# Node-weight products in units of four PSUM banks, with the full-array and half-array passes in alternating order

## The chip, the cores and the metric

One core of one Trainium2 chip runs the whole kernel. The metric is the device time in microseconds (us). The engines have one instruction queue each and meet through semaphores: PE (matmuls, with its weight loads shown apart as PEld), DVE (vector), ACT (scalar) and POOL (general-purpose). PSUM, where the matmuls write, has eight banks of 128 x 512 float32.

## The reference, cut to what matters

Four layers of a graph network run one after the other on a state of 8 batches x 1024 nodes x 64 features, each followed by a residual sum and a layer norm. The change lies in the third:

```python
    def _L2_gnn_ref(x, A, embedding, weight, bias):
        w = jnp.einsum('nd,dkio->nkio', embedding, weight)     # (1024, 3, 64, 64)
        b = jnp.einsum('nd,do->no', embedding, bias)
        As = [jnp.eye(N, dtype=x.dtype), A]
        As.append(2.0 * (A @ As[-1]) - As[-2])
        x_g = jnp.einsum('knm,bmc->bnkc', jnp.stack(As, 0), x)
        out = jnp.einsum('bnki,nkio->bno', x_g, w)
        return out + b
...
    x = _layernorm(x + _L2_gnn_ref(x, adj, L2_gnn_embedding, L2_gnn_weight, L2_gnn_bias), axis=-1)
```

Each node has weights of its own, a mix of D = 16 weight matrices by its embedding. The kernel does not build them. It multiplies the three inputs x, A x and A A x by all 16 matrices and then sums the 16 results of 64 columns, each scaled by the node's embedding value.

## The kernel before

The nodes lie in NT = 8 tiles of 128. For each tile t the work goes in units j. A unit is one matmul target: some batches times one half (dh) of the 16 matrices, which is 8 matrices x 64 = 512 columns, one PSUM bank for each batch. Before, a unit has two batches and so two banks, and a tile has UNITS = 8 units, of which the function `products` (L1646 to L1665) makes one at a time.

Every value is split into a high and a low part in a reduced float format, so one float32 product is three passes (high x high, high x low, low x high). The inputs x and A x of a batch stand together as 128 rows: they need three **full-array** passes for each bank (KH, KL against WH, WL: L1654 to L1656). The third input, A A x, has only 64 rows for each batch (GH, GL: L1664). Two batches, in the upper and in the lower half of the array, run as a pair of **half-array** passes at the same time. So a unit before is 6 full passes followed by 3 pairs of half passes.

The full passes need x and A x turned (features on the partitions). `turn(t)` (L1637) has PE transpose the 8 batches into two banks, 8 transposes from the buffer XX. ACT copies the two banks to KH (L1490, `turned`), DVE subtracts KH from the banks for KL (L1551, `low_parts`), and ACT then fills XX for the next tile (L1475, L1476, `inputs`).

What a unit leaves in its banks is taken out by two engines in turn. DVE's `accumulate` adds five of the eight groups of 64 columns, scaled, into X3, one chained instruction after the other (L1564). Then, `act.wait_ge(acc_step, DV * (u + 1))`, ACT's `scaled` writes the other three, scaled, to the ring SY (L1503). POOL sums the SY entries (L1432, L1435) and adds that sum to X3 once per tile (L1441, `combine`). PE's `banks_free` waits until ACT has taken out the unit that last used the same banks.

The order is written out by hand in the list `rounds`, which all engines follow: the turn of tile t + 1 stands between units 3 and 4 of tile t. Banks go round in four pairs, so PE is up to three units ahead of the one whose banks it takes back:

```python
        def pair_of_banks(t, j):
            at = 2 * (rounds.index((t, j)) % 4)
            return slice(at, at + 2)
```

Between the units ACT and DVE also do the layer norm of finished tiles: DVE takes statistics (L140) and makes scales, POOL makes the reciprocal roots (L163), ACT's `apply_norm` scales and shifts groups of 64 columns (L1510, two of them after a unit) and `next_high` (L1514) and DVE's `next_low` (L1577) make the inputs of the last layer. That layer's matmuls (L1705) begin when all 8 tiles are normed.

Of the kernel before, what the change touches and what calls it, by code (L numbers as in the profile page):

```python
# [9 lines left out]
ALU = mybir.AluOpType  # L10
# [6 lines left out]
F = 64  # L17
# [45 lines left out]
def program(nc, x_nat, x_tr, adj_tr, h_nat, h_tr, consts, weights, w01, w2, emb_bias, out):  # L63
    ctx = ExitStack()
    with ctx:
# [1044 lines left out]
        with nc.Block() as block:  # L1110
# [264 lines left out]
        kT_ready, k_h, k_l, y_ready, acc_step, sy_ready, yp_step, x3_sum = (  # L1375
            sem(s) for s in ("kT_ready", "k_h", "k_l", "y_ready", "acc_step", "sy_ready", "yp_step", "x3_sum"))
# [7 lines left out]
        UNITS = 2 * BP  # L1384
        SYS = 8
        SY = sb("SY", [P, SYS, 2 * F])
# [8 lines left out]
        def pair_of_banks(t, j):  # L1395
            at = 2 * (rounds.index((t, j)) % 4)
            return slice(at, at + 2)
# [9 lines left out]
        with nc.Block() as block:  # L1407
            @block.gpsimd
            def _(pool):
# [14 lines left out]
                def add_scaled(t, q):  # L1424
                    acc = YP[t % 2][:, tile(q)]
                    for i in range(1, 2 * DA):
                        n = 2 * DA * (BP * t + q) + i
                        pool.wait_ge(sy_ready, n + 1)
                        if i == 1:
                            if t >= 2:  # L1430
                                pool.wait_ge(x3_sum, t - 1)
                            ins = pool.tensor_tensor(acc, SY[:, (n - 1) % SYS, :], SY[:, n % SYS, :], ALU.add)  # L1432
                        else:
                            pool.wait_ge(yp_step, yp_steps(n - 1))
                            ins = pool.tensor_tensor(acc, acc, SY[:, n % SYS, :], ALU.add)  # L1435
                        ins.then_inc(yp_step, 1)

                def combine(t):
                    pool.wait_ge(acc_step, DV * unit(t + 1, 0))
                    pool.wait_ge(yp_step, yp_steps(2 * DA * BP * (t + 1) - 1))  # L1440
                    pool.tensor_tensor(X3[:, t, :], X3[:, t, :], YP[t % 2], ALU.add).then_inc(x3_sum, 1)  # L1441
# [7 lines left out]

                init(0)  # L1450
                for t in range(NT):
                    for q in range(BP):
                        add_scaled(t, q)
                        if q == 1:
                            for i, (first, n) in enumerate(NORMS):
                                if first + n == t:
                                    scales(i)
                        if q == 2 and t + 1 < NT:
                            init(t + 1)
                    combine(t)  # L1460
# [3 lines left out]
            def _(act):  # L1464
# [7 lines left out]
                def inputs(t):  # L1472
                    if t >= 1:
                        act.wait_ge(kT_ready, t)
                    act.activation(XX[:, :, 0, :], groups(X2[:, t, :]), ACT.Copy).then_inc(xx_ready, 1)  # L1475
                    act.activation(XX[:, :, 1, :], groups(XA[:, t, :]), ACT.Copy).then_inc(xx_ready, 1)  # L1476

                inputs(0)
                for i in range(2 * BP):
                    act.wait_ge(a2_ready, i + 1)  # L1480
                    act.activation(GH[:, i // 2, (i % 2) * HALF:(i % 2 + 1) * HALF], PS[:, 2 + i % 2, :], ACT.Copy,
                                   scale=2.0).then_inc(g_h, 1)
# [12 lines left out]
                def scaled(t, j):  # L1495
                    u = unit(t, j)
                    act.wait_ge(acc_step, DV * (u + 1))
                    for d in range(DV, DH):
                        n = DA * u + d - DV
                        if n >= SYS:  # L1500
                            act.wait_ge(yp_step, yp_steps(n - SYS))
                        e = W_EMB + t * D + (j % 2) * DH + d
                        act.activation(groups(SY[:, n % SYS, :]), PS[:, pair_of_banks(t, j), d * F:(d + 1) * F], ACT.Copy,  # L1503
                                       scale=WT[:, e:e + 1]).then_inc(sy_ready, 1)
# [11 lines left out]
                for t, j in rounds:  # L1516
                    if j is None:
                        turned(t)
                    else:
                        scaled(t, j)  # L1520
                        for i in range(3):
                            k = unit(t, j) - (16 * i + 22)
                            if 0 <= k < 8:
                                apply_norm(i, 2 * k, 2)
                            if k in (4, 8):
                                next_high(2 * i + k // 4 - 1)
# [6 lines left out]
            def _(dve):  # L1533
# [7 lines left out]
                for i in range(2 * BP):  # L1541
                    dve.wait_ge(g_h, i + 1)
                    c = slice((i % 2) * HALF, (i % 2 + 1) * HALF)
                    dve.scalar_tensor_tensor(GL[:, i // 2, c], PS[:, 2 + i % 2, :], 2.0, bits(GH[:, i // 2, c]),
                                             ALU.mult, ALU.subtract).then_inc(g_l, 1)

                def low_parts(t):
                    at = pair_of_banks(t, None).start
                    for h in range(2):
                        dve.wait_ge(k_h, 2 * t + h + 1)  # L1550
                        dve.tensor_tensor(KL[:, t % 2, 4 * h:4 * h + 4, :], PS[:, at + h, :].rearrange("p (b c) -> p b c", c=P),  # L1551
                                          bits(KH[:, t % 2, 4 * h:4 * h + 4, :]), ALU.subtract).then_inc(k_l, 1)

                def accumulate(t, j):
                    u, q, dh = unit(t, j), j // 2, j % 2
                    acc = groups(X3[:, t, tile(q)])
# [3 lines left out]
                    for d in range(DV):  # L1560
# [3 lines left out]
                        dve.scalar_tensor_tensor(acc, PS[:, pair_of_banks(t, j), d * F:(d + 1) * F], WT[:, e:e + 1], acc,  # L1564
# [14 lines left out]
                for t, j in rounds:  # L1579
                    if j is None:  # L1580
                        low_parts(t)
                        continue
                    accumulate(t, j)
                    if t >= 1 and j == 1:
                        statistics(t - 1)
                    if j == 2:
# [3 lines left out]
                    for i in range(3):  # L1590
                        k = unit(t, j) - (16 * i + 22)
                        if k in (6, 9):
                            next_low(2 * i + k // 3 - 2)
# [6 lines left out]
            def _(pe):  # L1600
# [8 lines left out]
                for i in range(2 * BP):  # L1609
                    q, c = i // 2, slice((i % 2) * HALF, (i % 2 + 1) * HALF)  # L1610
                    acc = PS[:, 2 + i % 2, :]
# [16 lines left out]
                def banks_free(t, j):  # L1628
                    i = rounds.index((t, j))
                    if i < 4:  # L1630
                        return
                    was_t, was_j = rounds[i - 4]
                    if was_j is None:
                        pe.wait_ge(k_l, 2 * was_t + 2)
                    else:
                        pe.wait_ge(sy_ready, DA * (unit(was_t, was_j) + 1))

                def turn(t):
                    at = pair_of_banks(t, None).start
                    banks_free(t, None)  # L1640
# [4 lines left out]

                def products(t, j):  # L1646
                    q, dh, r = j // 2, j % 2, t % 2
                    at = pair_of_banks(t, j).start
                    c = slice(dh * DH * F, (dh + 1) * DH * F)
                    banks_free(t, j)  # L1650
                    pe.wait_ge(k_l, 2 * t + q // 2 + 1)
                    for par in range(2):
                        b, acc = 2 * q + par, PS[:, at + par, :]
                        pe.matmul(acc, KH[:, r, b, :], WH[:, 0, c], start=True, stop=False, skip_group_check=True)  # L1654
                        pe.matmul(acc, KH[:, r, b, :], WL[:, 0, c], start=False, stop=False, skip_group_check=True)  # L1655
                        pe.matmul(acc, KL[:, r, b, :], WH[:, 0, c], start=False, stop=False, skip_group_check=True)  # L1656
                    if t == 0 and dh == 0:
                        pe.wait_ge(g_l, 2 * q + 1)
                    if t == 4 and j == 0:
                        pe.wait_ge(g_l, 2 * BP)  # L1660
                    for g, w in ((GH, WH), (GH, WL), (GL, WH)):
                        for par in range(2):
                            rows = slice(F * par, F * par + F)
                            ins = pe.matmul(PS[:, at + par, :], g[rows, q, tile(t)], w[rows, 1, c],  # L1664
                                            start=False, stop=(g is GL), skip_group_check=True)  # L1665
# [186 lines left out]
```

## Time and profile before

| | |
|---|---|
| timed runs, median of 3 | 905.51 us (902.73 to 907.22) |
| the profiled execution: its own time | 904.9 us |
| its span in the trace | 903.1 us |
| PE busy | 754.8 us, 84% of the span |
| DVE, ACT, POOL busy | 479.8, 345.5, 289.3 us |
| mean granted clock of PE | 0.907 of full speed |
| stretch of the units, from the first product to the last | 626.84 to 791.3 us of the span |

A matmul's duration in the trace covers its way through the array, and the next one starts before it ends. The time that a matmul costs is therefore read from one start to the next. "Idle before" in brackets is the time for which the engine stood still ahead of a row, and the name behind the arrow is what it waited for.

### The profile page before, as it was taken

The numbers are of one execution on the slowest core, as the hardware profiler recorded it, in microseconds if no ns is written. First come the engines' busy times: TensorE is split into PE (matmuls) and PEld (weight loads), VectorE is DVE, ScalarE is ACT, GpSimd is POOL, SyncE is SP. The second block draws the span as 40 slices with busy tenths as digits, with TensorE's granted clock in tenths as the row PEclk, the third lists the DMA queues.
The fourth block names the chain that finished last, engine by engine and source line by source line (L and its number), as shares of the span: only waits on it lengthen the run. The fifth ranks groups of instructions, "written<-read, shape, count | busy, mean of one in ns | idle before, by whom it ended". The sixth has DMA issues, their size and how long they took to land. (4 is left out here: it accounts for less than half of the span.)

```text
span 903.1 us, 10528 instructions
## 1 busy us (share of the span) xinstructions
PE 754.8 (84%) x3510; PEld 495.1 (55%) x3518; DVE 479.8 (53%) x1158; ACT 345.5 (38%) x724; POOL 289.3 (32%) x337
## 2 busy tenths in 40 slices
PE   3966977888898459899898993999999999939990
PEld 3646765666565358433232322787666666628880
DVE  1494254777357831245464666312778878820165
ACT  1741213545463121346353542222445564642110
POOL 0440001445446320001003149000556576730055
PEclk9967995999997579989998996899999999969995
DMA  8200011000000000000000001000000000000013
GB/s 277 70 24 1 1 32 62 2 1 0 1 1 1 0 1 1 1 0 1 1 0 1 0 5 45 1 1 1 1 1 0 1 1 1 1 0 1 1 24 70
DMA packets 12952, 14.39 MB, mean 16 GB/s; under 512 B 9680, under 2 KB 9680, under 8 KB 12896
## 3 DMA queue, kind: packets, MB, share of 16 engines
q1 hardware_dynamic: 11408, 11.61, 4.1%
q10 hardware_dynamic: 1488, 2.06, 0.7%
q8 instruction: 32, 0.52, 0.2%
q14 instruction: 24, 0.20, 0.1%
HBM read 11.57 MB, written 2.10 MB: 15 GB/s over the span
## 5 line engine op out<-in xcount | busy, mean ns | idle before, releaser
L1564 DVE SCALAR_TENSOR_TENSOR arena<-PS,WT,arena 128x128 f32<-128x128 f32 x320 | 111.2, 350 | 20.2 <-PE PS L1664 9.3
L1329 DVE TENSOR_REDUCE arena<-PS 128x1 f32<-128x1024 f32 x64 | 75.6, 1219 | 79.7 <-PE PS L1165 79.7
L1252 ACT ACTIVATE arena<-PS,arena 128x1024 f32<-128x1024 f32 x64 | 70.8, 1109 | 74.9 <-DVE arena L1329 74.9
L1503 ACT ACTIVATE SY<-PS,WT 128x128 f32<-128x128 f32 x192 | 56.5, 365 | 78.3 <-DVE arena L1564 78.3
L163 POOL TENSOR_TENSOR LN_Y<-LN_V,CN 128x16 f32<-128x16 f32 (+1 forms) x17 | 51.0, 2998 | 104.8 <-DVE LN_V L155 104.8
L1165 PE MATMUL PS<-arena 64*128 64x512 f32 x256 | 79.2, 636 | 4.6 <-ACT arena L1252 2.4
L1272 POOL TENSOR_TENSOR arena<-arena 128x128 f32<-128x128 f32 x32 | 12.9, 403 | 191.6 <-DVE arena L1333 191.6
L1183 PE MATMUL PS<-arena 128*64 128x512 f32 x256 | 64.2, 625 | 1.2 <-POOL arena L1272 1.1
L1654 PE MATMUL PS<-WH,KH 128*128 128x512 f32 x128 | 57.1, 446 | 1.4 <-DVE KL L1551 1.4
L1165 PEld LDWEIGHTS PS<-arena 64*128 64x128 f32 x256 | 28.9, 190 | 52.3 <-issue 33.4
L1655 PE MATMUL PS<-WL,KH 128*128 128x512 f32 x128 | 50.5, 395 | 0.0
L1656 PE MATMUL PS<-WH,KL 128*128 128x512 f32 x128 | 49.9, 390 | 0.0
L1705 PE MATMUL PS<-ADJH,NH 128*128 128x512 f32 x128 | 33.7, 407 | 15.2 <-PEq L1407 15.2
L1183 PEld LDWEIGHTS PS<-arena 128*64 128x64 f32 x256 | 16.3, 141 | 46.8 <-issue 44.4
L908 POOL TENSOR_TENSOR arena<-arena,CC 128x512 f32<-128x512 f32 x24 | 25.0, 1042 | 43.5 <-DVE arena L787 43.5
L1654 PEld LDWEIGHTS PS<-WH,KH 128*128 128x128 f32 x128 | 24.0, 187 | 25.3 <-issue 12.5
L140 DVE BATCH_NORM_STATS2 LN_ST<-arena 128x6 f32<-128x64 f32 x256 | 35.2, 209 | 3.4 <-POOL arena L1441 3.0
L1041 PE MATMUL PS<-arena,WT 128*128 128x512 f32 x64 | 36.0, 716 | 0.0
L1705 PEld LDWEIGHTS PS<-ADJH,NH 128*128 128x128 f32 x128 | 24.6, 197 | 20.5 <-issue 15.7
L1435 POOL TENSOR_TENSOR AGBD<-AGBD,SY 128x128 f32<-128x128 f32 x64 | 29.5, 461 | 18.7 <-ACT SY L1503 11.1
L895 POOL TENSOR_TENSOR HPL<-arena,HPH 128x512 fp32r<-128x512 f32 x8 | 10.2, 1279 | 78.6 <-ACT HPH L825 78.6
L1435 POOL TENSOR_TENSOR YP<-YP,SY 128x128 f32<-128x128 f32 x64 | 30.0, 469 | 16.5 <-ACT SY L1503 8.5
(263 smaller groups left out, 1608.0 us busy)
## 6 DMA issues: line engine op xcount, KB each, us to landing
arena<-in_adj_tr SPq DMA_DIRECT2D x8, 512.0 KB, 8.3
arena<-in_x_tr SPq DMA_DIRECT2D x4, 512.0 KB, 9.3
arena<-in_x_nat SPq DMA_DIRECT2D x1, 2048.0 KB, 8.3
out<-arena SPq DMA_DIRECT2D x8, 256.0 KB, 3.0
arena<-in_w SPq DMA_DIRECT2D x2, 512.0 KB, 4.1
WT<-in_weights ACTq DMA_DIRECT2D x1, 739.0 KB, 8.6
arena<-in_h_tr ACTq DMA_DIRECT2D x2, 256.0 KB, 10.8
CN<-in_consts ACTq DMA_DIRECT2D x1, 507.0 KB, 5.2
```

Of the source, the lines that this page charges most:

```text
L163: pool.tensor_tensor(LN_Y[:, at:at + n], LN_V[:, at:at + n], CN[:, C_NEGH:C_NEGH + n], ALU.pow).then_inc(ln_rstd, 1)
L1165: ins = pe.matmul(banks("S", 2 * i + par)[:, half, :], KT[q % 2][r, tile(m)], QT[q % 2][r, c], start=True, stop=True)
L1183: ins = pe.matmul(PS[r, 6 + half, :], AVN[:, i % RING, par, :], EF[2 * (i % RING) + par][:, c], start=(m == 0), stop=(m == NT - 1), skip_g ...
L1252: act.activation(EF[2 * (i % RING) + par], banks("S", 2 * i + par).rearrange("p a c -> p (a c)"), ACT.Exp, bias=NMX[:, i, par:par + 1], ac ...
L1329: dve.tensor_reduce(NMX[:, i, par:par + 1], banks("S", 2 * i + par), AX.XY, ALU.max, negate=True).then_inc(max_ready, 1)
L1435: ins = pool.tensor_tensor(acc, acc, SY[:, n % SYS, :], ALU.add)
L1503: act.activation(groups(SY[:, n % SYS, :]), PS[:, pair_of_banks(t, j), d * F:(d + 1) * F], ACT.Copy, scale=WT[:, e:e + 1]).then_inc(sy_rea ...
L1564: dve.scalar_tensor_tensor(acc, PS[:, pair_of_banks(t, j), d * F:(d + 1) * F], WT[:, e:e + 1], acc, ALU.mult, ALU.add).then_inc(acc_step, 1)
L1654: pe.matmul(acc, KH[:, r, b, :], WH[:, 0, c], start=True, stop=False, skip_group_check=True)
L1655: pe.matmul(acc, KH[:, r, b, :], WL[:, 0, c], start=False, stop=False, skip_group_check=True)
L1656: pe.matmul(acc, KL[:, r, b, :], WH[:, 0, c], start=False, stop=False, skip_group_check=True)
L1705: pe.matmul(acc, NH[:, m, tile(q)], ADJH[:, m, c], start=(m == 0), stop=False, skip_group_check=True)
```

## The change

A unit becomes four batches and four banks, so that a tile has four units (UNITS = BP = 4) and the banks go round in two sets, banks 0 to 3 for even units and 4 to 7 for odd ones. Each instruction of DVE, ACT and POOL that takes out or sums a unit handles 256 columns in place of 128, in half as many instructions. The ring SY keeps its size in bytes: 4 entries of twice the width. Even units do the 12 full passes first and then the 6 pairs of half passes, odd units the half passes first. The turn of tile t + 1 stands between units 1 and 2 of tile t and goes to banks 2 and 3, which unit 2 is about to fill. ACT copies both banks to XX in one instruction (semaphore k_raw), makes KH from XX in a second, and the subtraction for KL moves to POOL. XX for the next tile but one is filled after unit 3. `apply_norm` does four groups after a unit.

```diff
-        UNITS = 2 * BP
-        SYS = 8
-        SY = sb("SY", [P, SYS, 2 * F])
+        UNITS = BP
+        SYS = 4
+        SY = sb("SY", [P, SYS, 4 * F])
...
-            rounds += [(t, j) for j in range(4)] + ([(t + 1, None)] if t + 1 < NT else []) + [(t, j) for j in range(4, UNITS)]
+            rounds += [(t, j) for j in range(2)] + ([(t + 1, None)] if t + 1 < NT else []) + [(t, j) for j in range(2, UNITS)]
...
+        def four_banks(t, j):
+            at = 4 * (j % 2)
+            return slice(at, at + 4)
+
+        turn_banks = slice(2, 4)
...
+                def low_parts(t):
+                    pool.wait_ge(k_h, t + 1)
+                    pool.tensor_tensor(KL[:, t % 2, :, :], XX[:, :, :, :].rearrange("p b k f -> p b (k f)"), bits(KH[:, t % 2, :, :]), ALU.subtract).then_inc(k_l, 1)
...
+                low_parts(0)
                 init(0)
                 for t in range(NT):
...
+                    add_scaled(t, 0)
+                    for i, (first, n) in enumerate(NORMS):
+                        if first + n == t:
+                            scales(i)
+                    if t + 1 < NT:
+                        low_parts(t + 1)
+                        init(t + 1)
+                    add_scaled(t, 1)
                     combine(t)
...
                 def turned(t):
-                    at = pair_of_banks(t, None).start
+                    raw = XX[:, :, :, :].rearrange("p b k f -> p b (k f)")
                     act.wait_ge(kT_ready, t + 1)
                     if t >= 2:
                         act.wait_ge(y_ready, unit(t - 1, 0))
-                    for h in range(2):
-                        act.activation(KH[:, t % 2, 4 * h:4 * h + 4, :], PS[:, at + h, :].rearrange("p (b c) -> p b c", c=P),
-                                       ACT.Copy).then_inc(k_h, 1)
-                    if t + 1 < NT:
-                        inputs(t + 1)
+                    act.activation(raw, PS[:, turn_banks, :].rearrange("p a (b c) -> p (a b) c", c=P), ACT.Copy).then_inc(k_raw, 1)
+                    act.wait_ge(k_raw, t + 1)
+                    act.activation(KH[:, t % 2, :, :], raw, ACT.Copy).then_inc(k_h, 1)
...
                         scaled(t, j)
+                        if j == 3 and t + 2 < NT:
+                            inputs(t + 2)
                         for i in range(3):
-                            k = unit(t, j) - (16 * i + 22)
-                            if 0 <= k < 8:
-                                apply_norm(i, 2 * k, 2)
+                            k = unit(t, j) - (8 * i + 11)
+                            if 0 <= k < 4:
+                                apply_norm(i, 4 * k, 4)
...
-                def banks_free(t, j):
...
+                def banks_free(u):
+                    if u >= 2:
+                        pe.wait_ge(sy_ready, DA * (u - 1))
...
+                def two_terms(t, j, first):
+                    g, dh = j // 2, j % 2
+                    c = slice(dh * DH * F, (dh + 1) * DH * F)
+                    pe.wait_ge(k_l, t + 1)
+                    for i in range(4):
+                        if j == 2 and i == 2 and t + 1 < NT:
+                            pe.wait_ge(k_raw, t + 2)
+                        b, acc = 4 * g + i, PS[:, four_banks(t, j).start + i, :]
+                        passes = ((KH, 0, WH), (KH, 0, WL), (KL, 0, WH))
+                        for n, (x, k, w) in enumerate(passes):
+                            ins = pe.matmul(acc, x[:, t % 2, b, :], w[:, k, c], start=(first and n == 0),
+                                            stop=(not first and n == 2), skip_group_check=True)
+                    return ins
...
                 def products(t, j):
...
+                    banks_free(unit(t, j))
+                    if j % 2 == 0:
+                        two_terms(t, j, True)
+                        ins = third_term(t, j, False)
+                    else:
+                        third_term(t, j, True)
+                        ins = two_terms(t, j, False)
                     ins.then_inc(y_ready, 1)
```

`third_term` holds the half passes of L1664 in the same pairs, for p = 0 and 1. Nothing outside this stage is changed.

On PE, in order of issue, this is the turn of tile 1 inside tile 0 before: the end of unit 3, the turn and the beginning of unit 4. L1654 to L1656 are full passes, L1664 pairs of half passes, L1643 the 8 transposes.

```order
L1654 MATMUL PS<-WH,KH 128x512
L1655 MATMUL PS<-WL,KH 128x512
L1656 MATMUL PS<-WH,KL 128x512
L1664 MATMUL PS<-WH,GH 128x512 x2
L1664 MATMUL PS<-WL,GH 128x512 x2
L1664 MATMUL PS<-WH,GL 128x512 x2
L1643 MATMUL PS<-CN,XX 128x128 x8
L1654 MATMUL PS<-WH,KH 128x512
L1655 MATMUL PS<-WL,KH 128x512
L1656 MATMUL PS<-WH,KL 128x512
```

And this is the same place now: the last full passes of unit 1, the turn (L1641), and the first of unit 2, whose two first banks take the six full passes (L1654) shown here; the wait for k_raw stands behind the sixth.

```order
L1654 MATMUL PS<-WL,KH 128x512
L1654 MATMUL PS<-WH,KL 128x512
L1641 MATMUL PS<-CN,XX 128x128 x8
L1654 MATMUL PS<-WH,KH 128x512
L1654 MATMUL PS<-WL,KH 128x512
L1654 MATMUL PS<-WH,KL 128x512
L1654 MATMUL PS<-WH,KH 128x512
L1654 MATMUL PS<-WL,KH 128x512
L1654 MATMUL PS<-WH,KL 128x512
```

The half passes have gone from both sides of the turn. Six full passes of unit 2 now stand between the turn and the two banks that hold its result.

On ACT, this is the beginning of the stage before: the copies to KH for tile 0 (L1490), XX for tile 1, four units of SY (12 instructions), and then the turned inputs of tile 1.

```order
L1490 ACTIVATE KH<-PS 128x512 x2
L1475 ACTIVATE XX<-arena 128x8x64
L1476 ACTIVATE XX<-arena 128x8x64
L1503 ACTIVATE SY<-PS,WT 128x128 x12
L1490 ACTIVATE KH<-PS 128x512 x2
```

And now: two copies in a chain (L1499, L1501), XX for tile 1, two units of SY (L1511, 6 instructions), and the copies for tile 1.

```order
L1499 ACTIVATE XX<-PS 128x1024
L1501 ACTIVATE KH<-XX 128x1024
L1485 ACTIVATE XX<-arena 128x8x64
L1486 ACTIVATE XX<-arena 128x8x64
L1511 ACTIVATE SY<-PS,WT 128x256 x6
L1499 ACTIVATE XX<-PS 128x1024
L1501 ACTIVATE KH<-XX 128x1024
```

The copy that empties the turn's banks (L1499) still stands behind all SY instructions of the unit that PE finished just before the turn, and these are now unit 1 of four banks where they were unit 3 of two.

## Rows read from the trace of the kernel before

**Rows 1.** Windows: busy time by engine, instructions in brackets, from first product to last

```profile
core 0: us, PE busy (x) PEld busy (x) DVE busy (x) ACT busy (x) POOL busy (x), PEclk, DMA share, GB/s
626.84:791.30 164.46, 164.45 (x824) 104.01 (x824) 132.62 (x419) 87.24 (x269) 100.16 (x177) 1.00 0.00 1
```

**Rows 2.** Timeline of PE, unit 3 of tile 0 and the turn of tile 1

```profile
start us, us, engine line op out<-in xcount [idle before <-releaser]
634.27 0.50 PE L1654 MATMUL PS<-WH,KH 128*128 128x512 f32 x1
634.61 0.40 PE L1655 MATMUL PS<-WL,KH 128*128 128x512 f32 x1
634.85 0.39 PE L1656 MATMUL PS<-WH,KL 128*128 128x512 f32 x1
...
635.86 0.50 PE L1664 MATMUL PS<-WH,GH 64*128 64x512 f32 x2
636.19 0.40 PE L1664 MATMUL PS<-WL,GH 64*128 64x512 f32 x2
636.43 0.39 PE L1664 MATMUL PS<-WH,GL 64*128 64x512 f32 x2
636.75 1.09 PE L1643 MATMUL PS<-CN,XX 128*128 128x128 f32 x8
637.60 0.47 PE L1654 MATMUL PS<-WH,KH 128*128 128x512 f32 x1
```

**Rows 3.** Timelines of DVE and ACT behind that same unit 3

```profile
636.87 1.89 DVE L1564 SCALAR_TENSOR_TENSOR arena<-PS,WT,arena 128x128 f32<-128x128 f32 x5 [0.59 <-PE PS L1664]
...
638.79 0.88 ACT L1503 ACTIVATE SY<-PS,WT 128x128 f32<-128x128 f32 x3 [1.59 <-DVE arena L1564]
639.56 0.60 ACT L1490 ACTIVATE KH<-PS 128x512 fp32r<-128x512 f32 x1
```

**Rows 4.** Groups by line and shape, whole span: count, busy us, mean ns

```profile
L1564 DVE SCALAR_TENSOR_TENSOR arena<-PS,WT,arena 128x128 f32<-128x128 f32 x320 | 111.2, 350 | 20.2 <-PE PS L1664 9.3
L1544 DVE SCALAR_TENSOR_TENSOR GL<-PS,GH 128x512 fp32r<-128x512 f32 x8 | 5.5, 691 | 22.9 <-ACT GH L1481 22.9
L1503 ACT ACTIVATE SY<-PS,WT 128x128 f32<-128x128 f32 x192 | 56.5, 365 | 78.3 <-DVE arena L1564 78.3
L355 ACT ACTIVATE arena<-PS,WT 128x256 f32<-128x256 f32 x2 | 0.8, 470 | 0.0
L1738 ACT ACTIVATE arena<-PS 128x1024 f32<-128x1024 f32 x8 | 8.2, 1024 | 57.9 <-PE PS L1710 57.9
L1435 POOL TENSOR_TENSOR AGBD<-AGBD,SY 128x128 f32<-128x128 f32 x64 | 29.5, 461 | 18.7 <-ACT SY L1503 11.1
L1421 POOL TENSOR_TENSOR arena<-arena,BO 128x512 f32<-128x512 f32 x8 | 10.3, 1288 | 31.6 <-ACT XX L1476 31.6
L283 POOL TENSOR_TENSOR ADJL<-arena,ADJH 128x1024 fp32r<-128x1024 f32 x8 | 19.7, 2486 | 43.5 <-ACT ADJH L295 43.5
```

**Rows 5.** Windows around idle stretches of PE, with the granted clock (PEclk)

```profile
436.57:439.37 2.80, 0.01 (x1) 0.00 (x0) 2.75 (x4) 2.28 (x4) 0.40 (x1) 1.00 0.00 0
439.37:444.80 5.43, 5.43 (x12) 1.45 (x12) 0.00 (x0) 1.13 (x2) 0.00 (x0) 0.69 0.00 0
479.60:482.44 2.84, 0.04 (x1) 0.00 (x1) 2.78 (x4) 2.29 (x4) 2.25 (x4) 0.88 0.00 0
482.44:489.20 6.76, 6.76 (x12) 1.94 (x12) 0.00 (x0) 1.13 (x2) 0.30 (x1) 0.54 0.01 2
625.40:626.84 1.44, 0.03 (x1) 0.00 (x1) 1.26 (x3) 1.37 (x3) 0.00 (x0) 1.00 0.00 0
```

**Rows 6.** Timeline of PE, the turn of tile 0 and the first product

```profile
624.39 1.03 PE L1643 MATMUL PS<-CN,XX 128*128 128x128 f32 x8
626.84 0.50 PE L1654 MATMUL PS<-WH,KH 128*128 128x512 f32 x1 [1.41 <-DVE KL L1551]
```

**Rows 7.** Timelines of POOL and ACT at the end of the stage

```profile
793.71 1.64 POOL L1435 TENSOR_TENSOR YP<-YP,SY 128x128 f32<-128x128 f32 x3 [1.06 <-ACT SY L1503]
795.50 1.26 POOL L1441 TENSOR_TENSOR arena<-arena,YP 128x512 f32<-128x512 f32 x1
...
794.03 2.76 ACT L1510 ACTIVATE arena<-arena,LN_B,LN_Y 128x64 f32<-128x64 f32 x8
```

More of the change, by code:

```diff
@@ L1392, in program, with four @@
         for t in range(NT):
[L1393 to L1397 removed]
+            rounds += [(t, j) for j in range(2)] + ([(t + 1, None)] if t + 1 < NT else []) + [(t, j) for j in range(2, UNITS)]
[3 more added lines that the diff above has]
+        turn_banks = slice(2, 4)
+        def four(g):
+            return slice(g * 4 * F, (g + 1) * 4 * F)
         def unit(t, j):
@@ L1422, in init, with add_scaled @@
                                        BO[:, t:t + 1, :].broadcast_to([P, B, F]), ALU.add).then_inc(x3_init, 1)
-                def add_scaled(t, q):
-                    acc = YP[t % 2][:, tile(q)]
+                def low_parts(t):
+                    pool.wait_ge(k_h, t + 1)
+                    pool.tensor_tensor(KL[:, t % 2, :, :], XX[:, :, :, :].rearrange("p b k f -> p b (k f)"), bits(KH[:, t % 2, :, :]), ALU.subtract).then_inc(k_l, 1)
+                def add_scaled(t, g):
+                    acc = YP[t % 2][:, four(g)]
                     for i in range(1, 2 * DA):
-                        n = 2 * DA * (BP * t + q) + i
+                        n = 2 * DA * (2 * t + g) + i
                         pool.wait_ge(sy_ready, n + 1)
@@ L1502, in scaled @@
                         e = W_EMB + t * D + (j % 2) * DH + d
-                        act.activation(groups(SY[:, n % SYS, :]), PS[:, pair_of_banks(t, j), d * F:(d + 1) * F], ACT.Copy,
+                        act.activation(groups(SY[:, n % SYS, :]), PS[:, four_banks(t, j), d * F:(d + 1) * F], ACT.Copy,
                                        scale=WT[:, e:e + 1]).then_inc(sy_ready, 1)
@@ L1543, in _ @@
                     c = slice((i % 2) * HALF, (i % 2 + 1) * HALF)
-                    dve.scalar_tensor_tensor(GL[:, i // 2, c], PS[:, 2 + i % 2, :], 2.0, bits(GH[:, i // 2, c]),
+                    dve.scalar_tensor_tensor(GL[:, i // 2, c], PS[:, 4 + i % 2, :], 2.0, bits(GH[:, i // 2, c]),
                                              ALU.mult, ALU.subtract).then_inc(g_l, 1)
[L1547 to L1552, printed above, removed]
                 def accumulate(t, j):
-                    u, q, dh = unit(t, j), j // 2, j % 2
-                    acc = groups(X3[:, t, tile(q)])
+                    u, g, dh = unit(t, j), j // 2, j % 2
+                    acc = groups(X3[:, t, four(g)])
                     if j == 0:
@@ L1580, in _ @@
                     if j is None:
-                        low_parts(t)
                         continue
                     accumulate(t, j)
-                    if t >= 1 and j == 1:
+                    if t >= 1 and j == 0:
                         statistics(t - 1)
-                    if j == 2:
+                    if j == 1:
                         for i, (first, n) in enumerate(NORMS):
@@ L1590, in _ @@
                     for i in range(3):
-                        k = unit(t, j) - (16 * i + 22)
-                        if k in (6, 9):
-                            next_low(2 * i + k // 3 - 2)
+                        k = unit(t, j) - (8 * i + 11)
+                        if k in (2, 4):
+                            next_low(2 * i + k // 2 - 1)
                 statistics(NT - 1)
@@ L1626, in _ @@
                 pe.wait_ge(wl_ready, 2)
-                def banks_free(t, j):
[L1629 to L1636, printed above, removed]
+                def banks_free(u):
+                    if u >= 2:
+                        pe.wait_ge(sy_ready, DA * (u - 1))
                 def turn(t):
-                    at = pair_of_banks(t, None).start
-                    banks_free(t, None)
+                    at = turn_banks.start
+                    banks_free(unit(t, 0) - 2 if t else 0)
                     pe.wait_ge(xx_ready, 2 * t + 2)
@@ L1644, in turn @@
                     ins.then_inc(kT_ready, 1)
-                def products(t, j):
[L1647 to L1665, printed above, removed]
@@ new lines, in third_term @@
+                def third_term(t, j, first):
+                    g, dh = j // 2, j % 2
+                    c = slice(dh * DH * F, (dh + 1) * DH * F)
+                    if t == 0 and j < 2:
+                        pe.wait_ge(g_l, 2 * BP if j else 3)
+                    for p in range(2):
+                        for n, (x, w) in enumerate(((GH, WH), (GH, WL), (GL, WH))):
+                            for par in range(2):
+                                rows = slice(F * par, F * par + F)
+                                ins = pe.matmul(PS[:, four_banks(t, j).start + 2 * p + par, :], x[rows, 2 * g + p, tile(t)], w[rows, 1, c],
+                                                start=(first and n == 0), stop=(not first and n == 2), skip_group_check=True)
+                    return ins
```

28 lines of the change are left out of this document (11 added, 17 removed).

## The prediction

> **What bounds the kernel now.** I read the page's slices first: around 630 to 790 us of the span PE is busy all the time and its clock is full. One window over the stage says it exactly [rows 1]: from the first product at 626.84 to the last at 791.3 us PE is busy for 164.45 of 164.46 us at a granted clock of 1.00, DVE for 132.6, ACT for 87.2, POOL for 100.2. So here only PE's own issue counts, and the next question is what it spends its time on. The timeline of one unit answers that [rows 2]: the unit begins at 634.27, the turn at 636.75, so a unit takes 2.48 us. Within it a full pass follows a full pass after 0.24 us or a little less (634.61, 634.85), and one pair of half passes the other after 0.24 (636.19, 636.43). Yet the first pass of each kind is followed only after 0.33 to 0.34 us (634.27 to 634.61, 635.86 to 636.19), and the last half pair is followed by the turn after 0.32. Nine slots of 0.234 us are 2.11 us. The 0.37 that is left belongs to the two changes of kind, 0.185 us each. Check: 64 units of 2.48 and 7 turns of 0.85 (636.75 to 637.60) are 164.7 us, against 164.5 in the trace. There are no other waits to win.
>
> The second thing to read is what stands behind a unit [rows 3]. The turn is issued at 636.75, DVE starts at 636.87, its five chained instructions take 1.89 us, ACT starts 0.03 us later, its three take 0.88, and the copy of the turned inputs starts 0.11 us before they end, at 639.56. Before, this costs PE nothing: it has four pairs of banks, and while ACT is still at unit 3 it works on units 4 and 5.
>
> **The change, part by part.** *Fewer changes of kind.* A unit is now 12 full passes and 6 pairs of half passes, 18 slots, and since the order alternates only one change is left in it: 18 x 0.234 + 0.185 = 4.40 us [rows 2]. Thirty-two of them are 140.8 us. The turn now stands between full passes; I keep 0.85 us for it and 0.08 for the slower pass behind it, 6.5 us for seven. Together 147.3 us, which is **17.2 us less**. Bounds: the passes and their count are the same as before, so nothing beyond the changes of kind can be saved.
>
> *Wider instructions of DVE, ACT and POOL.* None of these shapes stands in this stage, so I take them between rows [rows 4]. DVE: 350 ns at 128 columns, 691 at 512; on the straight line 464 at 256, and up to 484 if the first 128 columns cost more in overhead; I take 475. The chain's pitch grows as the duration does, from 1.89 us for five to **2.52** (2.45 to 2.56). ACT: a scaled copy of 256 columns took 470 ns against 365 for 128, so three take 0.88 + 3 x 0.105 = **1.20 us**. POOL: 461 ns and 1288 at 512 give 737. A unit is then out of its banks 0.2 + 2.52 + 0.03 + 1.20 + 0.05 = 4.0 us after PE has ended it. (The 0.2 is the 0.12 of rows 3 plus the longer way of an odd unit's last full pass.) PE is by then 4.0 us into the next unit of 4.40, so in plain units there is no wait, with 0.4 us to spare. DVE has 4.40 - 2.52 = 1.9 us between units, and the statistics and scales that stand there are shorter.
>
> *The turn is the exception, and I expect the gain to go there.* Let PE end unit 1 of a tile at time 0. It makes the turn until 0.85 and the six full passes of unit 2's first two banks until 0.85 + 0.08 + 6 x 0.234 = 2.33. Then it stands before banks 2 and 3, which hold the turned inputs. ACT can only copy them after unit 1's SY, and that waits for DVE's chain: 0.2 + 2.52 + 0.03 + 1.20 - 0.11 = 3.84, plus the copy of 1024 columns, 1.02 us [rows 4], plus 0.05 = 4.92. So PE waits for **2.6 us** (the profile will call it about 2.4, since the last pass still runs). Behind PE stands everything: the rest of unit 2 and all later units. Seven turns: 18.2 us. At two of them (tiles 3 and 5) `apply_norm` with four groups stands on ACT between SY and the copy. Eight groups took 2.76 us [rows 7], so four add about 1.35 us each time, 2.7 us. Bounds for one wait: with DVE and ACT at their present 1.89 and 0.88 us it is 1.65, and with the upper ends of the durations 2.7. The Trainium skill, TensorEngine Tiling (Array Packing), section PSUM Bottleneck, warns that packing speeds up PE but not the emptying of PSUM. That speaks against this change, and the wait above is what it would look like.
>
> *The start.* Before, PE waits 1.41 us between the turn of tile 0 and the first product at 626.84 [rows 6]. Now ACT copies 1024 columns from the turn's end at 625.47 to 626.5, then again to KH until 627.6, and then POOL subtracts 128 x 1024, 2.49 us by the nearest row (the same operation and shape, L283) [rows 4]: first product at 630.15, **3.3 us later**. In later tiles the same subtraction is hidden by units 2 and 3: KH is ready at 4.92 + 1.02 = 5.9 us after unit 1, and PE comes to the next tile at 4.92 + 3.0 + 4.40 = 12.3. Of these 6.4 us the subtraction takes 2.49; what is left, 3.9, must hold POOL's backlog, the reciprocal roots above all, and anything over it would go onto PE.
>
> *The end.* After the last product DVE's chain is 0.63 us longer, the first SY entry 0.1, and POOL's three additions, 1.64 us now [rows 7], take 2 x 0.87 + 0.74 = 2.47. X3's last sum comes **1.6 us later** after the last product, and all of the last layer's start hangs on it.
>
> Without the clock: -17.2 + 18.2 + 2.7 + 3.3 + 1.6 = **+8.6 us**, which makes 913.5 from the profiled execution's 904.9.
>
> *The clock.* Before, PE never stops in this stage. Now it stops eight times. What a stop of that length does is seen elsewhere in the trace [rows 5]: after 2.80 us of idle PE was granted 0.69 of its clock over the next 5.43 us, a loss of 1.7 us at full clock; after another of 2.84, 0.54 over 6.76 us, a loss of 3.1; after 1.44 us, at the start of this very stage, nothing. These are its two levels, 1.2 and 2.4 GHz, in a mix. My stops (five of 2.4, two of 3.8, one of 4.7 us) are nearer to the ones that cost. I take 1.7 us for six of the eight, **10 us**; the bounds are 0 and 8 x 3.1 = 25. That makes **923.5 us**. The profiled execution lies 0.6 us under the median of the timed runs, which I leave as it is.
>
> **The rivals.** *The clock holds.* The stops at the turns are a little shorter than those that cost, and PE is dense on both sides. Then only the start and the two long ones cost: 913.5 to 917. For it: the 1.44 us stop. Against: two of two stops of 2.8 us. The Trainium skill, TensorE: Matmul & The Clock Gate, section Why this matters for your kernels, sets its limit for idle gaps above my 2.4 us and so is on this rival's side; the 2.80 us rows are already below that limit and fell.
>
> *The wait at the turn is short.* If the time of a DVE or ACT instruction were mostly fixed, so that 256 columns cost what 128 do, the wait would be 1.65 us, seven of them 11.6, the end only 0.8 longer, and the stops so near to 1.44 that the clock holds: 904.9 - 17.2 + 11.6 + 2.7 + 3.3 + 0.8 = 906, **not slower** by a measurable amount. The place is DVE's chain and ACT's SY at the seven turns; it decides from a wait of (17.2 - 2.7 - 3.3 - 1.6) / 7 = 1.4 us downwards for faster. Against it: 512 columns take twice the time of 128 in rows 4.
>
> *The clock falls hard.* If each stop costs like the second, 3.1 us, the sum is 913.5 + 25 = 938.
>
> **How the numbers follow.** Clock falls at most stops, 918 to 931: 0.58. Clock holds, 911 to 917: 0.22. Short wait, 899 to 910: 0.12, a third of it below 901. Harder fall or another wait, above 931: 0.08. The range leaves out the last two cases: 910 to 931. A measurement of this kernel can tell about 0.5%, 4.5 us, from no change: faster (under 901) 0.04, within (901 to 910) 0.08, slower 0.88.
>
> **What would show it.** In the profile after, PE stands still once in each of seven tiles, in front of the seventh full pass of unit 2, for about 2.4 us, twice 3.8, released by ACT's copy of 1024 columns. The passes of L1654 and L1667 must show 0.234 us from start to start and one change of 0.18 in each unit; a plain unit must last 4.40. DVE's five must take about 2.5 us, ACT's three 1.2. The first product must come 5.8 us after the turn of tile 0 begins. The granted clock must show falls behind some of the stops. Wrong would be: waits in front of other units (the 0.4 us to spare is not there), a DVE instruction far from 475 ns, or a clock that stays at 1.00.

## The result, and the profile after

The changed kernel takes 923.66 us (median of 4 runs, 922.41 to 925.05), the kernel before 904.12 us (median of 4, 902.12 to 907.22): its time is put at 1.0204 times the one before, 95% interval 1.0176 to 1.0232 (the two medians alone give 1.0216). It is slower clear of the noise, by about 2%. The profiled execution took 923.8 us with a span of 922.0; before it was 904.9 and 903.1.

The page of the changed kernel, its head:

```profile
span 922.0 us, 10016 instructions
PE 749.9 (81%) x3518; PEld 509.1 (55%) x3518; DVE 438.7 (48%) x982; ACT 336.7 (37%) x628; POOL 293.8 (32%) x265
```

PE is busy for 5 us less than before and the kernel is 19 us longer: PE's work did shrink, and PE stands still instead. Where it does is seen on the timeline of PE. These are the first product, then unit 1's last pass, the turn and unit 2 of tile 0 (in [rows 2] the turn at 636.75 had a product 0.85 us behind it and no stop), and then the first rows behind the stops of tiles 3 and 6:

```profile
630.05 0.80 PE L1654 MATMUL PS<-WH,KH 128*128 128x512 f32 x1 [4.62 <-POOL KL L1431]
...
641.05 0.39 PE L1654 MATMUL PS<-WH,KL 128*128 128x512 f32 x1
641.28 1.03 PE L1641 MATMUL PS<-CN,XX 128*128 128x128 f32 x8
642.07 0.47 PE L1654 MATMUL PS<-WH,KH 128*128 128x512 f32 x1
...
643.31 0.40 PE L1654 MATMUL PS<-WH,KL 128*128 128x512 f32 x1
646.25 0.50 PE L1654 MATMUL PS<-WH,KH 128*128 128x512 f32 x1 [2.54 <-ACT XX L1499]
...
712.37 0.80 PE L1654 MATMUL PS<-WH,KH 128*128 128x512 f32 x1 [3.91 <-ACT XX L1499]
...
780.70 0.50 PE L1654 MATMUL PS<-WH,KH 128*128 128x512 f32 x1 [2.60 <-ACT XX L1499]
```

There are seven such stops, one in each tile but the last, five of 2.54 to 2.60 us and two (tiles 3 and 5) of 3.91 and 3.90, 20.7 us together; each delays PE by 0.16 more than is shown, since the last pass still runs. The same place on DVE and ACT:

```profile
641.48 2.56 DVE L1569 SCALAR_TENSOR_TENSOR arena<-PS,WT,arena 128x256 f32<-128x256 f32 x5 [1.69 <-PE PS L1654]
...
644.08 1.21 ACT L1511 ACTIVATE SY<-PS,WT 128x256 f32<-128x256 f32 x3 [3.05 <-DVE arena L1569]
645.16 1.03 ACT L1499 ACTIVATE XX<-PS 128x1024 f32<-128x1024 f32 x1
```

The chain is as long as its parts: 2.56 us on DVE, 1.21 on ACT, 1.03 for the copy, where [rows 3] had 1.89 and 0.88 and nobody waited. The groups that answer to [rows 4]:

```profile
L1569 DVE SCALAR_TENSOR_TENSOR arena<-PS,WT,arena 128x256 f32<-128x256 f32 x160 | 77.4, 484 | 88.0 <-PE PS L1667 64.3 <-PE PS L1654 16.1 <-DVE LN_ST L140 2.9
L1511 ACT ACTIVATE SY<-PS,WT 128x256 f32<-128x256 f32 x96 | 38.6, 473 | 101.2 <-DVE arena L1569 101.2
L1444 POOL TENSOR_TENSOR AGBD<-AGBD,SY 128x256 f32<-128x256 f32 x32 | 23.6, 738 | 22.0 <-ACT SY L1511 18.2 <-POOL AGBD L1444 0.4
L1431 POOL TENSOR_TENSOR KL<-XX,KH 128x1024 fp32r<-128x1024 f32 x8 | 19.0, 2377 | 65.0 <-ACT KH L1501 65.0
```

DVE lost 34 us of work in this stage and gained nothing by it: it now waits for PE, and PE at each turn waits for ACT's copy, which stands behind DVE's own chain. The windows behind the start and behind the stops show the clock. Its column is the third from the end (1.00 is 2.4 GHz, half of it 1.2):

```profile
630.05:635.60 5.55, 5.55 (x14) 3.96 (x16) 0.00 (x0) 1.13 (x2) 1.18 (x1) 0.52 0.01 3
690.20:693.60 3.40, 3.40 (x18) 2.71 (x20) 0.57 (x2) 0.00 (x0) 3.32 (x3) 0.53 0.00 0
712.37:717.50 5.13, 5.13 (x18) 3.66 (x20) 0.00 (x0) 1.03 (x1) 3.60 (x2) 0.52 0.01 3
758.09:762.00 3.91, 3.91 (x12) 2.70 (x14) 0.00 (x0) 1.04 (x1) 2.79 (x2) 0.56 0.00 0
780.70:786.00 5.30, 5.30 (x26) 3.94 (x27) 0.63 (x2) 1.05 (x1) 5.10 (x4) 0.68 0.00 0
646.25:654.00 7.75, 7.75 (x44) 5.88 (x45) 2.56 (x6) 2.25 (x4) 5.18 (x5) 1.00 0.00 0
```

Five of the eight stops were followed by a fallen clock, the first five rows; the length of each window times what is missing from 1.00 makes 2.7 + 1.6 + 2.5 + 1.7 + 1.7 = 10.2 us. Behind the other three, as in the last row, it stayed whole.

### The profile page after: what moved, and what is told of

Read it like the earlier page. It is cut to its first block and busy times, and to the rows that moved or that the text cites. A ratio compares the mean times of both kernels' runs of the same rounds, so it can differ in the third digit from the quotient of the medians.

```text
span 922.0 us, 10016 instructions
## 1 busy us (share of the span) xinstructions
PE 749.9 (81%) x3518; PEld 509.1 (55%) x3518; DVE 438.7 (48%) x982; ACT 336.7 (37%) x628; POOL 293.8 (32%) x265
## 5 line engine op out<-in xcount | busy, mean ns | idle before, releaser
L1569 DVE SCALAR_TENSOR_TENSOR arena<-PS,WT,arena 128x256 f32<-128x256 f32 x160 | 77.4, 484 | 88.0 <-PE PS L1667 64.3
L1654 PE MATMUL PS<-WH,KH 128*128 128x512 f32 x128 | 55.3, 432 | 25.4 <-ACT XX L1499 20.7
L1511 ACT ACTIVATE SY<-PS,WT 128x256 f32<-128x256 f32 x96 | 38.6, 473 | 101.2 <-DVE arena L1569 101.2
L1654 PE MATMUL PS<-WH,KL 128*128 128x512 f32 x128 | 52.2, 408 | 0.0
L1654 PE MATMUL PS<-WL,KH 128*128 128x512 f32 x128 | 51.8, 405 | 0.0
L1654 PEld LDWEIGHTS PS<-WH,KH 128*128 128x128 f32 x128 | 24.9, 195 | 38.6 <-ACT XX L1499 23.8
L1431 POOL TENSOR_TENSOR KL<-XX,KH 128x1024 fp32r<-128x1024 f32 x8 | 19.0, 2377 | 65.0 <-ACT KH L1501 65.0
L1718 PEld LDWEIGHTS PS<-ADJH,NH 128*128 128x128 f32 x128 | 24.6, 197 | 22.1 <-issue 17.2
L895 POOL TENSOR_TENSOR HPL<-arena,HPH 128x512 fp32r<-128x512 f32 x8 | 10.2, 1281 | 78.6 <-ACT HPH L825 78.6
L283 POOL TENSOR_TENSOR ADJL<-arena,ADJH 128x1024 fp32r<-128x1024 f32 x8 | 19.7, 2487 | 43.4 <-ACT ADJH L295 43.4
```

The source lines that it names most:

```text
L1511: act.activation(groups(SY[:, n % SYS, :]), PS[:, four_banks(t, j), d * F:(d + 1) * F], ACT.Copy, scale=WT[:, e:e + 1]).then_inc(sy_ready, 1)
L1569: dve.scalar_tensor_tensor(acc, PS[:, four_banks(t, j), d * F:(d + 1) * F], WT[:, e:e + 1], acc, ALU.mult, ALU.add).then_inc(acc_step, 1)
L1654: ins = pe.matmul(acc, x[:, t % 2, b, :], w[:, k, c], start=(first and n == 0), stop=(not first and n == 2), skip_group_check=True)
L1718: pe.matmul(acc, NH[:, m, tile(q)], ADJH[:, m, c], start=(m == 0), stop=False, skip_group_check=True)
```

## The experiments

Medians are of the timed runs. An interval behind a ratio is its 95% interval. Ratios are to the kernel before, whose runs on the same chip had medians of 905.45 us (e1 to e5) and 904.43 us (e6 to e8). "Stage" is the time from the first product to the end of the last in the profiled execution: 164.45 us before, 177.06 with the change.

**e1: ACT copies the turned inputs before it takes unit 1 out.** `turned` is split into `turned_raw` (the copy to XX) and `turned_high` (the copy to KH). On the changed kernel, in ACT's loop over the rounds:

```diff
                     if j is None:
-                        turned(t)
...
                     else:
+                        if j == 1 and t + 1 < NT:
+                            turned_raw(t + 1)
                         scaled(t, j)
+                        if j == 1 and t + 1 < NT:
+                            turned_high(t + 1)
```

> The changed kernel, but ACT copies the turned inputs out of banks 2 and 3 before it takes unit 1's SY out, and makes KH after them. Theory: the seven stops come from that copy's place behind DVE's chain and ACT's SY of unit 1. Ahead of them it can end 0.85 + 0.15 + 1.03 + 0.05 = 2.1 us after unit 1, and PE comes to the banks at 2.3. All seven stops go (21.9 us by the trace of after), and with them the four clock falls behind them (about 7 us): 923.7 - 29 = 895 us. Rival (emptying is the bound: DVE and ACT need 4.0 us for each unit of four banks, and any delay shows elsewhere): the stop moves to the next units, because unit 1's SY is later by the copy; 905 to 915 us, with waits of PE on SY.

Measured: 905.45 us, ratio 0.9999 (0.9984 to 1.0015); stage 158.2 us. That is 18 us off the changed kernel, but not the expected 895. The number lies at the lower end of the rival's 905 to 915, but the rival's waits for SY are not there. What is left of the stops, on the timeline of PE:

```profile
630.70 0.80 PE L1662 MATMUL PS<-WH,KH 128*128 128x512 f32 x1 [4.62 <-POOL KL L1431]
689.97 0.47 PE L1662 MATMUL PS<-WH,KH 128*128 128x512 f32 x1 [1.83 <-POOL KL L1431]
703.01 0.50 PE L1662 MATMUL PS<-WH,KH 128*128 128x512 f32 x1 [0.25 <-ACT XX L1498]
730.64 0.47 PE L1662 MATMUL PS<-WH,KH 128*128 128x512 f32 x1 [1.82 <-POOL KL L1431]
743.67 0.50 PE L1662 MATMUL PS<-WH,KH 128*128 128x512 f32 x1 [0.27 <-ACT XX L1498]
771.32 0.47 PE L1662 MATMUL PS<-WH,KH 128*128 128x512 f32 x1 [1.80 <-POOL KL L1431]
```

The long stops for ACT's copy are gone, with 0.25 and 0.27 us left in tiles 3 and 5, where `apply_norm` is ahead of it. In their place PE waits three times for POOL's KL at the beginning of a tile. What POOL did ahead of the first of these waits:

```profile
681.82 2.52 POOL L1444 TENSOR_TENSOR AGBD<-AGBD,SY 128x256 f32<-128x256 f32 x3 [2.35 <-ACT SY L1514]
684.30 2.91 POOL L163 TENSOR_TENSOR LN_Y<-LN_V,CN 128x16 f32<-128x16 f32 x1
687.28 0.22 POOL L1457 TENSOR_TENSOR LN_B<-LN_M,LN_Y 128x16 f32<-128x16 f32 x1
687.47 2.36 POOL L1431 TENSOR_TENSOR KL<-XX,KH 128x1024 fp32r<-128x1024 f32 x1
```

The subtraction stands behind the additions and the reciprocal root. The clock behind the three waits:

```profile
689.97:694.50 4.53, 4.53 (x14) 3.30 (x14) 0.73 (x2) 3.17 (x8) 4.01 (x5) 0.62 0.00 0
730.64:735.00 4.36, 4.36 (x12) 3.17 (x12) 0.75 (x2) 3.00 (x8) 3.93 (x5) 0.61 0.02 4
771.32:776.00 4.68, 4.68 (x28) 3.61 (x30) 0.77 (x3) 2.64 (x7) 4.11 (x6) 1.00 0.00 0
```

It fell behind the waits of 1.83 and 1.82 us, for a loss of 1.7 us each, and not behind the one of 1.80. The waits (5.5 us) and the two falls (3.4) are 8.9 of the 10.5 us that are missing from the expected gain. In the changed kernel the stop at the turn had held PE back by 2.6 us and so hidden that POOL is late.

**e3: each unit does its full passes and then its half passes.**

```diff
-                    if j % 2 == 0:
-                        two_terms(t, j, True)
-                        ins = third_term(t, j, False)
-                    else:
-                        third_term(t, j, True)
-                        ins = two_terms(t, j, False)
+                    if t == 0 and j == 1:
+                        pe.wait_ge(g_l, 2 * BP)
+                    two_terms(t, j, True)
+                    ins = third_term(t, j, False)
```

> The changed kernel without the alternating order: each unit does its full passes and then its half passes, so a unit has two changes of kind and not one. Theory: a change of kind costs PE 0.17 to 0.19 us, and PE's issue sets the time between the stops: 32 changes more (31 between units, less the seven at the turns that were none, plus those) are 5.4 to 6.1 us: 929.5 us. Rival (it is the larger unit that saves, the order does not matter; or the extra time hides in the 0.4 us that a unit's emptying leaves): 923.7 us.

Measured: 927.2 us (923.94 to 930.56), ratio 1.0242 (1.0205 to 1.0278). The stage is 182.41 us, 5.35 longer. The interval overlaps that of the changed kernel, so the timed runs alone do not settle it; the stage does: PE's busy time in it is 162.6 us against 177.06 - 20.7 = 156.4, which is 6.2 more for 32 more changes of kind, 0.19 each. Some 0.4 us of the 6.2 is the clock, which fell behind five of the seven stops and not four; that leaves 0.18 each.

**e4: the kernel before, with the order alternating, in units of two banks.** The six full and six half passes are as before; in `products`:

```diff
+                    if dh == 0:
+                        full(True)
+                        ins = half(False)
+                    else:
+                        half(True)
+                        ins = full(False)
```

> The kernel before, with units of two banks, where units with the second half of the matrices (dh = 1) do the half passes first; nothing else is changed. Theory: changes of kind fall from 128 to 64 at 0.18 us each, and PE never waits in this stage, so the whole saving shows: 904.1 - 11.8 = 892.3 us. Rival (a unit now ends sooner than DVE and ACT can follow: they are 1.9 us a unit on DVE plus statistics and scales against 2.29 us of PE): part of it is given back as waits on SY, 897 to 900 us. Second rival (the cost of a change is hidden by weight loads): 904 us.

Measured: 900.92 us, ratio 0.9957 (0.9941 to 0.9974). The stage is 157.11 us, 7.3 shorter; PE is idle in it for 2.5 us, in seven waits for ACT's SY, of which the longest, 0.50 us, is shown under the window of the stage:

```profile
core 0: us, PE busy (x) PEld busy (x) DVE busy (x) ACT busy (x) POOL busy (x), PEclk, DMA share, GB/s
625.53:782.64 157.11, 154.57 (x824) 108.16 (x824) 130.13 (x412) 85.65 (x262) 97.49 (x171) 1.00 0.00 1
...
759.67 0.50 PE L1657 MATMUL PS<-WH,KH 128*128 128x512 f32 x1 [0.50 <-ACT SY L1503]
```

PE's busy time fell by 9.9 us for 64 changes of kind. That is a little too small a fall, since the 0.16 us for which the last pass runs into each of the seven waits counts as busy. At the end 2.7 us were lost: the last sum of X3 comes 8.2 us after the last product, against 5.5 before. DVE and POOL at that place, where the last product ends at 782.64:

```profile
781.62 5.69 DVE L1564 SCALAR_TENSOR_TENSOR arena<-PS,WT,arena 128x128 f32<-128x128 f32 x15
...
787.79 1.64 POOL L1435 TENSOR_TENSOR YP<-YP,SY 128x128 f32<-128x128 f32 x3 [0.50 <-ACT SY L1503]
```

DVE takes out the last three units in one piece, without a wait, and is done at 787.3; in the kernel before it had waited 0.58 us for the last unit and began on it 0.04 us after the last product. So the backlog is DVE's, with units that now come every 2.3 us. POOL is not what lasts longest: it waits for the last unit's SY. So the first rival is the one that held: a good part is given back by the engines that take out, though the time is 1 us above its 897 to 900.

**e5: the stops filled with matmuls.** In `two_terms`, ahead of the first pass, which overwrites the bank:

```diff
+                        if j == 2 and i == 0 and t + 1 < NT:
+                            for _ in range(17 if t in (3, 5) else 11):
+                                pe.matmul(acc, KH[:, t % 2, b, :], WH[:, 0, c], start=True, stop=True, skip_group_check=True)
```

> The changed kernel, with 11 more full-array matmuls (17 in tiles 3 and 5) into the first bank of unit 2 ahead of its passes, which overwrite them. They take 2.5 (3.9) us, so PE reaches the turned inputs' banks when these are being freed, and is busy where it stood still. Theory: the stops cost twice, once as idle time and once through the fallen clock; the filler leaves the first and takes the second away, 7 us by the cold stretches behind the stops in the trace of after: 917 us. Rival (the falls lie in time that something else hides): 923.7 us or, if the filler overshoots, above.

Measured: 914.93 us (911.62 to 918.94), ratio 1.0102 (1.0059 to 1.0144); stage 170.33 us, 6.7 shorter with 89 matmuls more. The window behind the slow start:

```profile
636.10:800.80 164.70, 164.02 (x901) 125.08 (x899) 91.28 (x244) 75.65 (x170) 101.84 (x105) 1.00 0.00 1
```

The granted clock is 1.00 throughout. PE comes to the seventh full pass of unit 2 when it did: in tile 0 it starts 4.98 us after the turn's start (641.67 to 646.65), against 4.97 in the changed kernel. Only the half-speed stretches are gone, and they were worth 6.7 us of the stage. The medians differ by 8.7, but the four runs lie apart, two at 912 and two at 918 to 919 us, and the profiled one (917.53) is of the upper two.

**e6: tile 0's turned inputs taken out as before.** ACT writes KH from the banks and DVE subtracts from the banks, both for tile 0 alone; the counts that are waited for on k_raw go down by one:

```diff
-                low_parts(0)
                 init(0)
...
+                            act.wait_ge(kT_ready, 1)
+                            act.activation(KH[:, 0, :, :], PS[:, turn_banks, :].rearrange("p a (b c) -> p (a b) c", c=P),
+                                           ACT.Copy).then_inc(k_h, 1)
...
+                dve.wait_ge(k_h, 1)
+                dve.tensor_tensor(KL[:, 0, :, :], PS[:, turn_banks, :].rearrange("p a (b c) -> p (a b) c", c=P),
+                                  bits(KH[:, 0, :, :]), ALU.subtract).then_inc(k_l, 1)
```

> The changed kernel with tile 0's turned inputs taken out as before: ACT writes KH straight from the banks, DVE makes KL from the banks; later tiles are as changed. Theory: the first product comes 2.3 us earlier or more (it was 3.2 us later than before, and ACT's single copy of 1024 columns and DVE's single subtraction cost a little against the two halves: 1.0 + 1.2 us after the turn, first product at 3.4 us from the turn's start against 5.65), and the clock does not fall there, which cost 2.6 us: 923.7 - 4.9 = 918.8 us. Rival (the clock falls after a stop of 2.3 us there too): 921.4 us.

Measured: 917.4 us (912.67 to 918.79), ratio 1.0131 (1.0100 to 1.0162). The first product comes 3.41 us after the turn's start, against 5.65 in the changed kernel and 2.45 before. The turn starts at 622.67:

```profile
626.08 0.50 PE L1661 MATMUL PS<-WH,KH 128*128 128x512 f32 x1 [2.37 <-DVE KL L1563]
```

The first product comes 2.2 us earlier, as expected. The median is near the expected 918.8, but the timed runs, which spread over 6 us, cannot choose between it and the rival's 921.4. The trace can. The window behind the first stop:

```profile
626.08:630.50 4.42, 4.42 (x12) 3.32 (x12) 0.00 (x0) 1.13 (x2) 0.00 (x0) 0.61 0.01 4
```

The clock fell behind this stop of 2.37 us too, for a loss of 1.7 us where it had been 2.7, so the rival had the mechanism right. Part of the rest is chance: at the turns the clock fell three times here and four times in the changed kernel.

**e7: e1 with POOL's subtraction ahead of its roots.**

```diff
                     add_scaled(t, 0)
+                    if t + 1 < NT:
+                        low_parts(t + 1)
                     for i, (first, n) in enumerate(NORMS):
                         if first + n == t:
                             scales(i)
                     if t + 1 < NT:
-                        low_parts(t + 1)
                         init(t + 1)
```

> e1_copy_first, with POOL's subtraction for KL ahead of its reciprocal roots in each tile. Theory: what kept e1 at 905 us and not 895 are three waits of 1.8 us of PE for KL, in the three tiles in which POOL takes a root of 2.9 us first, and two clock falls behind them (1.55 us each). KL then ends about 3.1 us earlier and all three waits go: 905.5 - 5.4 - 3.1 = 897 us. Rival (POOL is too full by now whatever its order: what it does late in a tile delays SY or X3's sums, and PE waits on ACT's SY): 900 to 905 us.

Measured: 894.05 us, ratio 0.9878 (0.9858 to 0.9898). The stage by a window:

```profile
629.43:779.08 149.65, 148.65 (x824) 112.29 (x824) 91.33 (x244) 76.54 (x172) 102.52 (x106) 0.98 0.00 1
```

No wait for KL is left after the first one; PE is idle for 1.0 us, in four waits of 0.16 to 0.29 for SY. The time is 3 us under the expected 897, and the rival's 900 to 905 is excluded.

**e8: e7 with the start of e6.** The two edits together.

> e7_pool_order with the start of e6_start_as_before: units of four banks and alternating order without the three costs found so far. Theory: 897 - 4.9 = 892 us, with no stop of PE over 0.5 us in the stage and a granted clock of 1.00; against the kernel before that is -18.5 us of issue, +1.0 at the start, +1.6 at the end, about +2 for what is left. Rival (the costs are not additive): 895 to 900 us.

Measured: 892.77 us (887.89 to 894.26), ratio 0.9859 (0.9835 to 0.9883), the fastest here, 12 us under the kernel before and close to the expected 892:

```profile
627.17:776.19 149.02, 148.06 (x824) 111.63 (x824) 91.29 (x244) 76.55 (x172) 101.26 (x105) 0.99 0.00 1
```

The clock of 0.99 comes from a fall behind the first wait, 2.37 us here as in e6, so the expected 1.00 was missed. Next to e7 the profiled execution gains 2.2 us at the start and 0.6 in the stage; in the timed runs the two intervals overlap.

## Why the prediction was right, step by step

The forecast was 923.5 us and slower, the measurement 923.66, with the case that was called likeliest. Its terms one by one, from the two traces:

*Fewer changes of kind, predicted -17.2.* e7 has the changed kernel's passes nearly without stops: 149.65 us, of which 1.0 is idle and 0.02 x 149.65 = 3.0 the fallen clock at the start, leaves 145.7 against 164.45, **-18.8**, or 0.195 us for each of 96 changes. It was read right, and a little small: a pass follows a pass of its kind after 0.23 us, and a plain unit lasts 4.31 us (unit 0 of tile 1, 653.66 to 657.97), where 4.40 was taken.

*The stops at the turns, predicted 18.2 + 2.7 = 20.9.* Idle 20.7 us, delay **21.9** with 0.16 for each. The row that the sum was least sure of was DVE's at 256 columns: 484 ns, the upper bound, where 475 was taken. e1 shows the cause: with ACT's copy moved ahead and nothing else, all long stops are gone. The rival of a short wait needed DVE's time to be fixed; it goes from 350 to 484 ns with twice the columns, and ACT's from 365 to 473, so it fell there.

*The start, predicted +3.3.* 5.65 us from the turn to the first product against 2.45: **+3.2**.

*The end, predicted +1.6.* The last sum of X3 ends at 814.16, 7.05 us after the last product; before it was 796.76 and 5.47: **+1.6**.

*The clock, predicted +10, 1.7 us at six of eight stops.* **10.2** by the granted clock: fewer falls, five, and two of them longer. So the mechanism was right, but that the sum came out is luck: the prediction had the number of falls and the loss at each wrong in opposite directions. e5 measured the part behind the turns by itself: 6.7 us of the stage, where the windows give 7.5. The rival of the held clock fell with it; in the timed runs e5 is 1.0102, above no change and below the changed kernel. The Trainium skill's limit for idle gaps (TensorE: Matmul & The Clock Gate, Why this matters for your kernels), which had been on that rival's side, does not hold as a safe limit here: the clock fell behind a stop of 2.60 us at 688.46, and again behind that at 780.70.

The terms add up to -18.8 + 21.9 + 3.2 + 1.6 + 10.2 = 18.1 us, against 18.9 in the span. In the stage alone they give 13.3 where the trace has 12.6, since a pass at half clock takes a little less than twice its time (0.43 us from start to start behind 630.64, against 0.23); the last layer, which nothing was forecast for, took 1.5 us more from its first matmul on (98.07 against 96.58), and in the other runs between 97.1 and 98.1. A hit within 0.2 us is better than the terms are: the saving was 1.6 us larger than predicted, the stops 1.0 and the last layer 1.5 us longer, and with the 0.7 us by which the terms overstate the stage these nearly cancel.

What the prediction did not have is what lay under the stops. It gave POOL 3.9 us beside the subtraction for its backlog and said that anything over it would reach PE. In the changed kernel nothing did. But those 3.9 us contained the 2.6 us of the stop itself: once e1 took it away, POOL was 1.8 us late in three tiles and 10 us of e1's expected gain stayed away. The prediction's "the rest is hidden" was true only as long as its own biggest loss was there.

## What to carry to other kernels

When a buffer is made larger, count how many units are in flight, not how many bytes: four pairs of banks let PE run two units past an emptying, two sets of four let it run none past a place where a third user (here the turned inputs) borrows half of a set. Before such a change is dropped, look at the queue order of the engine that releases the wait; here one copy moved ahead of three others, and one subtraction ahead of a root, turned +2.0% into -1.2%. And when a stall is removed, whatever was hidden under it is next: ask of each "hidden" item whether the cover is work or another wait.

## What the runs showed of the hardware

Going between full-array and half-array passes costs PE about 0.2 us each time, with units of two banks and of four. The steps from start to start show it: two of 0.32 to 0.34 us at each change, where the others are 0.23. The balances give 0.195 (e7) and 0.18 to 0.19 (e3); e4 gives 9.9 / 64 = 0.155 of busy time, or 0.17 with the 7 x 0.16 us that its waits hide.

A stop of 2.4 to 2.6 us at the same place in a dense stream sometimes leaves the clock whole and sometimes not. Of the short stops at the turns (2.36 to 2.60 us) the clock fell behind two of five in the changed kernel, one of five in e6 and three of five in e3; behind the long ones (3.77 to 3.92 us) it fell every time, six of six in those three runs. Shorter stops are not safe either: it fell behind two of the three of 1.80 to 1.83 us in e1, and behind the 2.37 us at the start of e6 and of e8. Behind the 1.41 us at the start of the kernel before and of e4 it did not.

The spread of the timed runs does not simply follow the stops. It is 6.6 us in e3, 6.1 in e6 and 2.6 in the changed kernel, but also 7.3 in e5 and 6.4 in e8, which have no such stops at the turns. What makes it was not tried.
